# Four heads' score products side by side in four PSUM banks, transposed probabilities in the dense products' banks, recurrence steps spread by work

## The reference

```python
q_word, k_word, v_word = jnp.split(word_hidden_states @ c_attn_w + c_attn_b, 3, axis=-1)
k = concat([img @ uk_w.T + uk_b, k_word]); v = concat([img @ uv_w.T + uv_b, v_word])
scores = einsum('bhqd,bhkd->bhqk', q, k) / sqrt(32)   # causal mask, then + attention mask
attn = softmax(scores);  out = einsum('bhqk,bhkd->bhqd', attn, v) @ c_proj_w + c_proj_b
x = x + out
step: next_h = tanh(prev_h @ Wh + x_t @ Wx + b)        # 512 steps in sequence, 8 sequences at once
x = x + hs
```

## Time and profile before

| | |
|---|---|
| median of 3 executions | 1738.16 us (1734.18 to 1741.51) |
| profiled execution: its time | 1743.1 us |
| profiled execution: its span | 1741.3 us, mean granted TensorE clock 0.976 |
| TensorE busy | 1654.6 us, 95% |
| VectorE, ScalarE, GpSimd busy | 798.4, 670.5, 184.6 us |
| chain that ended last | TensorE 89% |

### The profile page before, as it was taken

The page is one execution under the profiler, slowest core; times in us unless marked ns, Lnnn a source line. Parts: engine busy times, 40 slices in busy tenths (PEclk is TensorE's granted clock), DMA queues, the critical chain, the costliest instruction groups (busy, mean ns, idle before and its releaser), DMA issues.

```text
span 1741.3 us, 74131 instructions
## 1 busy us (share of the span) xinstructions
PE 1654.6 (95%) x32749; PEld 1263.7 (73%) x32749; DVE 798.4 (46%) x2687; ACT 670.5 (39%) x2257; POOL 184.6 (11%) x300
## 2 busy tenths in 40 slices
PE   6889999999999999999999999999999999999775
PEld 6667777787777778777777777777677677767654
DVE  3444444444445454454545455454554454544221
ACT  3433333433334334443434443443443443434111
POOL 2111010111011101101011110111100101100000
PEclk8868999999999999999999999999999999999998
DMA  6222121221223222232323333233332343321000
GB/s 234 78 52 65 42 57 51 63 67 56 57 59 87 62 75 68 82 88 73 85 66 98 89 85 93 60 103 98 88 98 73 103 108 94 92 69 35 15 9 14
DMA packets 167903, 130.24 MB, mean 75 GB/s; under 512 B 54264, under 2 KB 153112, under 8 KB 167072
## 3 DMA queue, kind: packets, MB, share of 16 engines
q1 hardware_dynamic: 153792, 92.92, 19.1%
q0 software_dynamic: 13792, 32.58, 6.7%
HBM read 100.00 MB, written 25.43 MB: 72 GB/s over the span
## 4 chain that ended last, share of the span: by engine, by line
PE 89%; issue 3%; DVE 2%; DMA 2%; ACT 2%; SPq 1%; POOL 0%; DVEq 0%; ACTq 0%; POOLq 0%
PE rec L1044 26%; PE scores L963 11%; PE turned L974 11%; PE dense L492 8%; PE dense L493 7%; PE dense L494 7%; PE rec L1035 6%; PE pv L991 5%; PE pv L1009 2%; PE scores L1044 2%; DVE pre L870 1%; ACT states L724 1%; PE dense L945 1%; PE dense L1051 1%; SPq L517 1%
## 5 line engine op out<-in xcount | busy, mean ns | idle before, releaser
L1044 PE MATMUL rec<-wh,states 128*32 128x128 f32 x15360 | 516.4, 275 | 27.0 <-ACT states L724 25.8
L1044 PEld LDWEIGHTS rec<-wh,states 128*32 128x32 f32 x15360 | 399.7, 110 | 123.3 <-ACT states L724 64.3
L676 ACT ACTIVATE probs<-probs,nmax 128x64 f32<-128x64 f32 (+7 forms) x512 | 271.6, 531 | 269.7 <-DVE nmax L815 266.6
L870 DVE STREAM_TRANSPOSE pre<-rec 128x128 f32<-128x128 f32 x480 | 151.7, 316 | 471.4 <-PE rec L1044 470.6
L724 ACT ACTIVATE states<-pre 128x32 f32<-128x32 f32 x512 | 133.1, 260 | 455.3 <-DVE pre L870 453.3
L815 DVE CUSTOM_DVE_ANT_0 probs<-scores,msk,nimg 128x64 f32<-128x64 f32 (+7 forms) x512 | 249.9, 514 | 62.8 <-PE scores L963 54.4
L974 PE MATMUL turned<-ident,probs 128*128 128x128 f32 (+1 forms) x1280 | 242.9, 292 | 7.9 <-ACT probsT L683 7.2
L963 PE MATMUL scores<-kt,q 32*64 32x64 f32 (+7 forms) x2048 | 231.4, 431 | 0.3 <-DVE nmax L815 0.2
L974 PEld LDWEIGHTS turned<-ident,probs 128*128 128x128 f32 (+1 forms) x1280 | 132.5, 135 | 90.4 <-issue 66.3
L824 DVE COPY probsT<-turned 128x128 f32<-128x128 f32 (+3 forms) x256 | 124.8, 487 | 78.4 <-PE turned L974 72.8
L683 ACT COPY probsT<-turned 128x128 f32<-128x128 f32 (+3 forms) x256 | 106.8, 417 | 115.3 <-PE turned L974 114.8
(11 more groups left out here) (148 smaller groups left out, 1817.4 us busy)
## 6 DMA issues: line engine op xcount, KB each, us to landing
vbuf<-v_dram SPq DMA_DIRECT2D x64, 192.0 KB, 2.8
xin<-x SPq DMA_DIRECT2D x64, 128.0 KB, 2.9
v_dram<-vbuf POOLq DMA_DIRECT2D x64, 128.0 KB, 2.7
out<-outs POOLq DMA_DIRECT2D x32, 256.0 KB, 4.2
vbuf<-v_dram SPq DMA_DIRECT2D x64, 128.0 KB, 2.4
kt<-k_dram SPq DMA_DIRECT2D x16, 512.0 KB, 4.1
vbuf<-v_dram SPq DMA_DIRECT2D x32, 256.0 KB, 3.4
k_dram<-knew POOLq DMA_DIRECT2D x60, 128.0 KB, 2.6
```

Source lines behind the costliest of these rows:

```text
L676: act.activation(probs[:, g % PROBS, 0:n], probs[:, g % PROBS, 0:n], ACT.Exp, scale=-1.0, bias=nmax[:, e, h:h + 1], accum_out=rowsum[:, e, ...
L870: dve.transpose(pre_all, rec_bank(g // GROUP)[:, 0:P]).then_inc(pre_ready, 1)
L1044: last = pe.matmul(rec_bank(g // GROUP)[Q * j:Q * j + Q, 0:P], state_tile(g - 1)[:, f, :], wh[:, f, P * j:P * j + P], start=False, stop=f ...
```

## The change

The scores of four heads are issued in one run, each head in a PSUM bank of its own, and no step is put inside a run. The two `turned` banks are gone: a turn is now a job in the rotation of the two dense banks, with the same wait for the copy of the job before it in the bank, and copies touch only rows that hold keys. The turn follows its score by 2 heads, not 4, and pv comes 2 heads earlier. `v` is emitted right behind `vfirst` where nothing was emitted in between. All 448 early steps are spread by weight over the whole stretch from the end of trip 1's projection to the start of trip 15's, with the condition that a step's part of x is ready.

```diff
-TURN_LAG = 4
-PV_LAG = 10
+TURN_LAG = 2
+PV_LAG = 8
...
@@ main_order @@
         if u < HEADS:
-            if u % 2 == 0:
-
-                emit([("score", v, 0, 0.07 + 0.107 * keys(g) / P) for v in (u, u + 1)])
+            if u % HC == 0:
+
+                emit([("score", v, 0, 0.06 + 0.06 * keys(g) / P) for v in range(u, u + HC)])
...
             share -= side[0][3]
             emit([side.pop(0)])
+            if out[-1][0] == "vfirst":
+                share -= side[0][3]
+                emit([side.pop(0)])
     return out
@@ order @@
-    for b in range(PARTS - 1):
-        first = ends[(b + 1) * QUADS - 1] + 1
-        for n in range(QUADS):
-
-            last = begins[(b + 1) * QUADS + n]
-            whole = sum(w for *_, w in main[first:last])
-            done, t = 0.0, 0
-            for at in range(first, last):
-                done += main[at][3]
-                while t < STEPS and (done >= whole * (t + 0.5) / STEPS or at + 1 == last):
-                    place.setdefault(at, []).append(b * W + n * STEPS + t)
-                    t += 1
-            first = last
+    first, last = ends[QUADS - 1] + 1, begins[TRIPS - 1]
+    whole = sum(w for *_, w in main[first:last])
+    done, t = 0.0, 0
+    for at in range(first, last):
+        done += main[at][3]
+        if main[at][0] == "score" and main[at][1] % HC < HC - 1:
+
+            continue
+
+        while (t < FIRST and at > ends[(t // W + 1) * QUADS - 1]
+               and (done >= whole * (t + 0.5) / FIRST or at + 1 == last)):
+            place.setdefault(at, []).append(t)
+            t += 1
@@ attention_recurrence @@
     for kind, g, i in ORDER["PE"]:
-        if kind in DENSE_KINDS and kind != "v":
+        if kind in DENSE_KINDS + ("turn",) and kind != "v":
             count = 2 if ("xsteps", 0, 0) in JOB else 3
...
-        scores = [ctx.enter_context(nc.psum_tensor(f"scores{i}", [P, BANK], F32)) for i in range(2)]
-        turned = [ctx.enter_context(nc.psum_tensor(f"turned{i}", [P, BANK], F32)) for i in range(2)]
+        scores = [ctx.enter_context(nc.psum_tensor(f"scores{i}", [P, BANK], F32)) for i in range(HC)]
...
-        turned_copied = [sem(f"turned_copied{i}") for i in range(2)]
...
+        def turns_copied(group):
+
+            return dict((JOB["turn", g, 0][0], JOB["turn", g, 0][1] + 1) for g in range(HC * group, HC * group + HC))
...
@@ scalar, turn (vector: the same with tensor_copy and turned[0]) @@
                     n = P * tiles_of(g // UNITS)
+                    rows = slice(0, min(P, keys(g // UNITS)))
...
-                    act.copy(probsT[:, g % TURNED, 0:n], turned[1][:, 0:n]).then_inc(turned_copied[1], 1)
+                    act.copy(probsT[rows, g % TURNED, 0:n], bank(kind, g, 0)[rows, 0:n]).then_inc(copied(kind, g, 0), 1)
@@ vector, score @@
-                    dve.tensor_tensor_reduce(out=probs[:, g % PROBS, 0:n], in0=scores[g % 2][:, 0:n],
+                    dve.tensor_tensor_reduce(out=probs[:, g % PROBS, 0:n], in0=scores[g % HC][:, 0:n],
@@ tensor, score @@
-                    if g > 1:
-                        pe.wait_ge(shifted_ready, g - 1)
+                    if g == 0:
+
+                        pe.wait_ge(image_ready, 1)
+                    if g >= HC:
+                        pe.wait_ge(shifted_ready, g - HC + 1)
...
-                        last = pe.matmul(scores[g % 2][W * b:W * b + W, 0:n], q[rows, trip % 2, c, at:at + W],
+                        last = pe.matmul(scores[g % HC][W * b:W * b + W, 0:n], q[rows, trip % 2, c, at:at + W],
@@ tensor, turn @@
-                    if g == 0:
-                        pe.wait_ge(image_ready, 1)
-                    if g > 1:
-                        pe.wait_ge(turned_copied[g % 2], g // 2)
+                    wait_bank(pe, kind, g, 0)
                     for at in range(0, n, P):
-                        last = pe.transpose(turned[g % 2][0:min(P, n - at), at:at + P],
+                        last = pe.transpose(bank(kind, g, 0)[0:min(P, n - at), at:at + P],
                                             probs[:, g % PROBS, at:min(at + P, n)], ident[:])
@@ tensor, pv @@
-                    for parity in range(2):
-                        pe.wait_ge(turned_copied[parity], 2 * g + 2)
+                    for held, count in turns_copied(g).items():
+                        pe.wait_ge(dense_copied[held], count)
```

More of the change, by code:

```diff
@@ L649, in _ @@
                 high_qkv(i)
-            for f, d in enumerate(scores + turned):
+            for f, d in enumerate(scores):
                 act.wait_ge(setup_turned, C + 2 + f)
@@ L775, in _ @@
                     dve.wait_ge(setup_product, 2)
-                    dve.tensor_tensor(vimg_all, turned[0][:, :], uvb, ALU.add).then_inc(image_ready, 1)
+                    dve.tensor_tensor(vimg_all, scores[0][:, :], uvb, ALU.add).then_inc(image_ready, 1)
                     dve.wait_ge(image_ready, 1)
@@ L823, in _ @@
                         dve.wait_ge(pv_done, (g - TURNED) // HC + 1)
-                    dve.tensor_copy(probsT[:, g % TURNED, 0:n], turned[0][:, 0:n]).then_inc(turned_copied[0], 1)
+                    dve.tensor_copy(probsT[rows, g % TURNED, 0:n], bank(kind, g, 0)[rows, 0:n]).then_inc(copied(kind, g, 0), 1)
                 elif kind == "imgprob":
@@ L933, in _ @@
                     for f in range(C):
-                        last = pe.matmul(turned[0][:, :], rbc[:, f, :], wh[:, f, :], start=f == 0, stop=f == C - 1)
+                        last = pe.matmul(scores[0][:, :], rbc[:, f, :], wh[:, f, :], start=f == 0, stop=f == C - 1)
                     last.then_inc(setup_product, 1)
```

## The result

The changed kernel takes 1811.95 us (median of 4 runs, 1808.76 to 1817.34); the kernel before, on the same chip, 1739.84 us (4 runs). The ratio is 1.042, with an interval of 1.038 to 1.046: **slower by 4.2%**, where 2.4% faster was forecast. The profiled execution took 1811.5 us with a span of 1809.7, 68.4 more than before (1741.3).

The account below looks back on a forecast made before the run. The prediction took TensorE to bound the kernel from 148 to 1592 us. Its terms: 1743.1 − 122 − 1 − 6 + 82 + 5 = 1701, as a median 1696 us (2.4% faster), range 1650 to 1750.

Parts of the forecast that it names:

- What bounds the kernel: From 148 to 1592 us TensorE is the bound: a microsecond taken from it is gained, unless it begins to wait.
- Part 1: Score products: groups fall from 313 to 128, four heads cost a pair's price and 0.03 us; 122 us saved.
- Part 2: Turns sharing the dense banks wait for copies held behind four shifts and exponentials; 82 us added.
- the walk: Step-by-step timing of TensorE, VectorE and ScalarE behind score runs, mainly trip 11 (6.5 us idle), used to set waits per trip.
- The upper bound: Highest estimate of added waits from turns in the dense banks: 1.3 us for each of 128 score runs, 166 us.
- what would upset everything: A change of the granted clock between 200 and 1500 us, where it stood at full 2.4 GHz; given no price.
- Part 3: pv directly behind norm in 16 of 32 cases waits 0.9 us for VectorE's scaling; counted inside the 82 us.
- Part 4: Steps spread over the stretch: 6 us of idle taken back, nine in a row from step 384 add 5 us.
- Part 5: vfirst and v together: only 4 of 32 end up as neighbours; worth 1 us.
- The queues as bound: Rival: VectorE's and ScalarE's queues bind behind each score run, 166 us of waits, median 1780 us; chance 0.13.
- Small waits: Rival: the lags leave enough room, only unavoidable places cost, 40 us; median 1654 us; chance 0.22.
- Four tiles at a time: Rival: only four score tiles run at once on TensorE, so 43 us are saved; median 1763 us; chance 0.07.

Follow-up runs that it names:

- Whole pairs: The kernel before, with no step put between the two heads of a score pair (256 groups of scores in place of 313): 1704.05 us against 1741.94, ratio 0.978.

## Why the prediction was wrong

**What bounds the kernel: right.** The profile said that a microsecond taken from TensorE is one gained as long as it does not begin to wait. Whole pairs show the first half, the changed kernel the second.

**Part 1, the score products: right.** 120 us saved, against 122 forecast; run prices 1.04 and 0.30 as forecast. Of it some 41 come from runs that are no longer split, and the pairs alone collect them without any wait.

**Part 2, turns in the dense banks: the step that failed.** The term of 82 us measured nearly 150, norm and pv included. Three things in it were off.

First, it priced only waits for a bank, and the place of norm. "Before, a copy of a turn could be late" was seen; that the turn itself needs its exponential, and that the lag falls from four heads to two, was not priced as a cost of its own. The lags alone cost 69 us, with 36.5 us of turns waiting for exponentials; some 21 of the 69 are norm and pv.

Second, the walk came out too low, at its own trip and more so at other sizes. In the two runs that it writes out it was right to 0.15 us. But trip 11 idles 10.0 us more than before where it summed 6.5, and trip 6 7.0 more (8.5 against 1.6) where it summed 3.8. The waits that the account shows as added came to 31 us in trips 0 to 5 where 15 were set, 29 in trips 6 to 9 where 17.6 were, and 67 in trips 10 to 15 where 49 were; and these are still without the 16 of norm and pv, which the 82 us included. (TensorE's idle time alone, with norm and pv in it, grew by 38, 30 and 79 us.) Over the whole program, pieces that the walk passed over in "small pieces" carry most: in the account steps go from 15 to 48 us, xsteps from 10 to 32, turns from 12 to 29, q and k products from 1 to 17. No run isolates why. The likely reason is a chain: a late tanh delays a step, this delays what stands behind it in TensorE's order, and the next run begins with less in hand.

Third, the slow side had too little weight. The upper bound, 1.3 us for each of 128 runs or 166 us, did hold: measured are 148/128, or 1.16 us a run. That is past the point from which the rival decides (124 us, some 1.0 us a run). The evidence against that rival, that six of eight runs of trip 11 cost much less, was taken from the same walk as the forecast, and so could not speak against it. It deserved far more than 0.13.

**The clock: left out of the sum, and wrong.** "I take no change of clock into the sum", and it added some 30 us. Before, the granted clock stood at the full level from 168 to 1605 us; now it fell 13 times between 190 and 1660 us. The rival's 1780 has no such term either, and is 32 us below the result. The text had named this as what would upset everything, but did not give it a price, although each forecast had 40 to 166 us of new waits in it.

**Part 3, pv right behind norm: right in kind and size.** 16 places at 0.95 us in the row, 0.9 forecast; moving norm gives back 20 us in the changed kernel and 21 with the lags alone.

**Part 4, steps: the burst came, the gain did not.** The first, second and last of the nine steps in TensorE's timeline:

```profile
1470.38 1.08 PE L1051 MATMUL rec<-wh,states 128*32 128x128 f32 x32
1472.18 1.08 PE L1051 MATMUL rec<-wh,states 128*32 128x128 f32 x32 [0.72 <-ACT states L730]
...
1486.64 1.06 PE L1051 MATMUL rec<-wh,states 128*32 128x128 f32 x32
```

16.3 us from the first to the ninth start, as forecast. The 6 us taken back in trips 2 to 5 were overrun by the new waits there; the spread as a whole gains nothing, and may cost up to 8 us.

**Part 5, v behind vfirst: forecast at 1 us, and not measured in the changed kernel.** Always joined it brings nothing in the kernel with whole pairs (9 us slower).

**The rivals.** The queues as bound came nearest. By the prediction's own sign, idle time of more than 130 us added between 148 us and the end of attention, it is this case: 151 us now (1513 less 1361.56), 18 before. VectorE is busy for 43% and ScalarE for 36% of the span, and yet TensorE waits for them. But runs of four are only half of it. With the same lags and banks and scores in pairs, waits already stand at 130 us in place of 63, and that half has no run of four behind it. Small waits (1654) were far off. Four tiles at a time is excluded by the two timelines of runs.

The Trainium skill, page "TensorEngine Tiling (Array Packing)", section "PSUM Bottleneck", says that tiling speeds up TensorE but not the copies out of PSUM, which may then become the bound. The runs agree in the outcome: going from pairs to fours took 66 us from TensorE and added 65 of waits. They differ in the manner, since neither copying engine is full by its busy share: the lags and the order of the burst, changed without any change of work, moved the time by 69 and 21 us.

## What to carry to other kernels

When an edit frees banks by shortening the distance between a product and its user, price the distance as a part of its own, in every link (score to exponential to turn to copy to pv), and try it alone first: here two constants cost 69 us. Look for the part of an optimization that shortens the bounding engine without touching any distance; not splitting pairs gave 38 us for two lines. And when the forecast has new waits on an engine whose granted clock is seen to fall behind waits, give the clock a term too.

## What the runs showed of the hardware

**The clock falls behind single waits, in a kernel that is 87% busy.** The windows around the split of x shown above (stretch, length, busy PE, PEld, DVE, ACT, POOL, granted clock, DMA):

```profile
981.90:989.40 7.50, 7.50 (x149) 6.49 (x149) 4.29 (x18) 3.99 (x13) 1.71 (x3) 1.00 0.28 64
989.40:991.90 2.50, 0.02 (x3) 0.00 (x0) 0.00 (x0) 0.02 (x1) 0.00 (x0) 1.00 1.01 235
991.90:998.70 6.80, 5.18 (x83) 3.74 (x83) 2.46 (x5) 1.60 (x5) 0.00 (x0) 0.50 0.35 108
```

TensorE worked without a gap until 989.4 us at 2.4 GHz and then stood idle for 4.1 us, until 993.5. Inside this gap, from 991.9 us on, it was granted 1.2 GHz for 6.8 us, of which it was busy for 5.18. In the changed kernel 13 such falls of 3.4 to 10.2 us lie between 190 and 1660 us, and over the whole span the lower level holds for 142 us in place of 85. Whole pairs show 60 us. It is not the sum of the waits alone that counts: with the banks alone TensorE idled for 129 us and the lower level held for 40, with the lags alone for 142 and 122. Between 165 us and the end of attention the longest single wait was 2.4 us with the banks, 3.6 with the lags and 4.1 in the changed kernel. But the length of a wait alone doesn't settle it either. A wait of 1.08 us:

```profile
1267.48 1.40 PE L998 MATMUL pv<-probsT,vbuf 128*32 128x64 f32 x64 [1.08 <-DVE x1T L855]
```

and one of 2.33 us:

```profile
1433.22 1.08 PE L1051 MATMUL rec<-wh,states 128*32 128x128 f32 x32 [2.33 <-ACT states L730]
```

and the windows behind the first and around the second, same columns as above:

```profile
1268.40:1271.80 3.40, 3.40 (x72) 2.95 (x74) 0.00 (x0) 0.00 (x0) 0.00 (x0) 0.50 0.30 87
1430.00:1445.00 15.00, 11.27 (x280) 8.27 (x273) 8.80 (x29) 9.48 (x28) 0.26 (x1) 1.00 0.47 152
```

The shorter wait was followed by a fall to 1.2 GHz, the longer one by none. What else decides, no run varied by itself.

**Eight tiles of 32 by 64 at once cost 0.03 us more than four**, in two row groups more: with 512 keys the median from start to next start is 1.044 us for eight and 1.018 for four. This had been open, since no row of the kernel before had more than four. The Trainium skill, page "TensorE: Matmul & The Clock Gate", section "Measured speedup vs the span model", gives about 4 ns for each further tile; the four further ones here cost 26 ns, 6.5 each, so somewhat more.
